# Mixer of a language-model tower: order of the second norm's root, the residual update and the sums behind the inverse

## The reference, cut to what matters

```
h = tok(x)                                   # ends in a layer norm with weights gf, bf
h = h + attn(layernorm(h))                   # the mixer
h = h + ffn(layernorm(h))                    # starts with a layer norm and a Fourier transform over the tokens

def attn(x):                                 # x is already layernorm(h)
    xn = (x - mean(x)) / sqrt(var(x) + 1e-5) * gamma + beta
    q, k, v = split(xn @ w_qkv)              # 16 features each
    q_l, k_l = means of 4 tokens of q, k     # 64 landmarks a sequence
    a1, a2, a3 = softmax(q k_l'), softmax(q_l k_l'), softmax(q_l k')
    z = a2' / (max column sum * max row sum)
    6 times: z = 0.25 z (13 I - a2 z (15 I - a2 z (7 I - a2 z)))
    out = a1 z (a3 v) + conv33(v)            # a convolution over tokens with 33 taps
    return x + out @ w_out + b_out
```

## Time and profile before

| | |
|---|---|
| three runs, us | 1111.16, 1113.62, 1119.43 (median 1113.62) |
| the profiled execution, us | 1112.04 |
| its span, first to last instruction, us | 1110.2 |
| TensorE busy | 973.0 us, 88% |
| VectorE, ScalarE, GpSimd busy | 606.5, 592.3, 426.6 us |
| mean granted TensorE clock | 0.927 of full |
| the mixer | from 491 to 604 us |

### The profile page before, as it was taken

One profiled execution on the slowest core, in us unless ns is written; L12 is line 12 of the kernel. 1 busy time (PEld: TensorE's weight loads), 2 busy tenths in 40 slices (PEclk: granted clock), 3 DMA queues, 4 the chain that ended last, 5 costly groups with the idle time before them and its releaser, 6 DMA issues. The chain is left out here.

```text
span 1110.2 us, 21063 instructions
## 1 busy us (share of the span) xinstructions
PE 973.0 (88%) x7350; PEld 709.2 (64%) x7350; DVE 606.5 (55%) x1802; ACT 592.3 (53%) x1332; POOL 426.6 (38%) x622
## 2 busy tenths in 40 slices
PE   2489999999999998625897999996899999997898
PEld 1256666667666665313685767775688888885564
DVE  4366776666766774135353111116277777784773
ACT  4166776676666766216434543326455555543476
POOL 6426777766677676548003000014400000027300
PEclk9699999999999999866698899998799999996899
DMA  4755444645554440010100011010000010005841
GB/s 131 170 104 132 94 93 108 151 107 110 118 127 94 94 97 8 1 33 0 47 3 9 20 36 32 21 33 1 20 10 11 11 54 15 1 1 136 214 100 37
DMA packets 54416, 71.82 MB, mean 65 GB/s; under 512 B 9476, under 2 KB 46624, under 8 KB 50464
## 3 DMA queue, kind: packets, MB, share of 16 engines
q1 hardware_dynamic: 53160, 67.33, 26.1%
q0 software_dynamic: 1152, 3.15, 1.2%
HBM read 48.96 MB, written 17.56 MB: 60 GB/s over the span
## 5 line engine op out<-in xcount | busy, mean ns | idle before, releaser
L2232 DVE TENSOR_REDUCE t_nmax<-banks 128x2 f32<-128x512 f32 x256 | 166.6, 685 | 86.7 <-PE banks L2042 81.4
L2161 ACT ACTIVATE t_probs<-banks 128x512 f32<-128x512 f32 x256 | 144.8, 592 | 78.9 <-PE banks L2064 77.8
L2042 PE MATMUL banks<-t_packed 96*128 96x256 bf16 x512 | 90.9, 278 | 15.0 <-DMA t_packed<-t_qk_pairs 12.9
L2320 POOL TENSOR_SCALAR xhat<-t_rbuf,mv,rstd 128x128 f32<-128x128 f32 x128 | 100.1, 795 | 3.3
L2064 PE MATMUL banks<-t_packed 120*128 120x256 bf16 x512 | 92.0, 278 | 9.3 <-DMA t_packed<-t_mT 8.6
L2042 PEld LDWEIGHTS banks<-t_packed 96*128 96x128 bf16 x512 | 47.4, 99 | 55.0 <-issue 27.1
L858 ACT ACTIVATE hid<-banks,b 128x512 f32<-128x512 f32 x64 | 43.5, 686 | 69.0 <-PE banks L763 68.3
L2064 PEld LDWEIGHTS banks<-t_packed 120*128 120x128 bf16 x512 | 46.7, 99 | 48.2 <-issue 21.2
L1192 ACT ACTIVATE l_probs<-banks,l_shift 128x256 f32<-128x256 f32 x128 | 59.4, 472 | 28.5 <-DVE l_shift L1233 25.8
L2077 PE MATMUL banks<-t_probs,t_v 128*32 128x256 f32 x1024 | 73.6, 392 | 0.6 <-ACT t_probs L2161 0.6
L901 DVE SCALAR_TENSOR_TENSOR acc<-banks,gates,acc 128x128 f32<-128x128 f32 (+1 forms) x72 | 20.1, 343 | 97.8 <-PE banks L783 97.8
(11 more groups left out here) (376 smaller groups left out, 2090.2 us busy)
## 6 DMA issues: line engine op xcount, KB each, us to landing
t_qk_pairs<-t_parts SPq DMA_DIRECT2D x32, 384.0 KB, 2.4
t_packed<-t_qk_pairs SPq DMA_DIRECT2D x32, 384.0 KB, 5.5
t_packed<-t_qk_pairs SPq DMA_DIRECT2D x32, 256.0 KB, 6.0
t_packed<-t_qk_pairs SPq DMA_DIRECT2D x32, 128.0 KB, 6.6
w<-in_L_ffn_w SPq DMA_DIRECT2D x16, 256.0 KB, 2.6
t_packed<-t_mT SPq DMA_DIRECT2D x32, 96.0 KB
g_qk_pairs<-g_parts SPq DMA_DIRECT2D x8, 384.0 KB, 5.7
g_packed<-g_qk_pairs SPq DMA_DIRECT2D x8, 384.0 KB, 4.8
```

The lines of the kernel that those rows point to most:

```text
L2042: ins = pe.matmul(m.mbank[:, n % 3, i * S:(i + 1) * S], m.packed[0:MROW, 0, p, h, c + qt * P:c + (qt + 1) * P], m.packed[0:MROW, 1, p, h, ...
L2161: act.activation(m.probs[:, n % 6, :], m.sbank[:, n % 2, :], ACT.Exp).then_inc(sem["probs_ready"], 1)
L2232: dve.tensor_reduce(m.nmax[:, b, u // 4, 2 * hp:2 * hp + 2], m.mbank[:, n % 3, :].rearrange("p (i k) -> p i k", i=2), AX.X, ALU.max, negat ...
L2320: ins = pool.tensor_scalar(m.xhat[:, k, i, :], m.rbuf[:, k, i, :], m.mv[:, k, i, 0:1], m.rstd[:, k, i:i + 1], ALU.subtract, ALU.mult)
```

## The change

Four things, all in the mixer:

1. The two roots of the second norm are computed apart. In H, GpSimd computes only the one that ScalarE's N needs (4 columns instead of 8, L587 and L588 of the changed kernel). The other one, 1 + root, the product and the residual update move into a new item NR (L590 to L598), which stands behind H 3 for pairs 0, 1 and 2 and behind SC for pair 3.
2. VO is cut in two (VT, VO), and ScalarE doesn't wait for the weights before the first F: VT comes behind F 2, F 3 behind H 0. N, NT, QK and VW of the four pairs are interleaved anew.
3. CV 0, which stood between VW 0 and QK 1, moves in front of CV 1, shortly before the inverse.
4. Behind the inverse, Y and R alternate pair by pair, and X, DF and HP are interleaved anew.

```diff
-    order = [("VO",)] + [("F", g) for g in range(PAIRS)]
-    order += [("H", 0), ("H", 1), ("N", 0), ("NT", 0), ("H", 2), ("N", 1), ("QK", 0), ("VW", 0), ("NT", 1), ("H", 3), ("N", 2), ("N", 3),
-              ("L", 0), ("CV", 0), ("QK", 1), ("NT", 2), ("NT", 3), ("S2", 0), ("L", 1), ("M2", 0), ("E2", 0), ("VW", 1),
-              ("QK", 2), ("QK", 3), ("A2", 0), ("S2", 1), ("L", 2), ("M2", 1), ("AT", 0), ("E2", 1), ("S31", 0), ("S2", 2), ("L", 3),
+    order = [("F", 0), ("F", 1), ("F", 2), ("VT",), ("H", 0), ("F", 3), ("VO",), ("H", 1), ("N", 0), ("NT", 0), ("H", 2), ("N", 1),
+             ("QK", 0), ("NT", 1), ("VW", 0), ("H", 3), ("NR", 0), ("NR", 1), ("NR", 2), ("N", 2), ("QK", 1), ("NT", 2), ("L", 0), ("N", 3), ("VW", 1),
+             ("S2", 0), ("QK", 2), ("NT", 3), ("L", 1), ("M2", 0), ("E2", 0), ("QK", 3),
+             ("A2", 0), ("S2", 1), ("L", 2), ("M2", 1), ("AT", 0), ("E2", 1), ("S31", 0), ("S2", 2), ("L", 3),
...
-              ("A2", 2), ("AT", 2), ("S31", 2), ("M31", 1), ("A2", 3), ("AT", 3), ("E31", 1), ("M31", 2), ("SC",), ("ET", 0), ("S31", 3),
-              ("E31", 2), ("M31", 3), ("VW", 2), ("CV", 1), ("E31", 3), ("VW", 3), ("ET", 1), ("P", 0), ("Z0",)]
+             ("A2", 2), ("AT", 2), ("S31", 2), ("M31", 1), ("A2", 3), ("AT", 3), ("E31", 1), ("M31", 2), ("SC",), ("NR", 3), ("ET", 0), ("S31", 3),
+             ("E31", 2), ("M31", 3), ("VW", 2), ("CV", 0), ("CV", 1), ("E31", 3), ("VW", 3), ("ET", 1), ("P", 0), ("Z0",)]
...
-    order += [("W2", g) for g in range(PAIRS)] + [("Y", g) for g in range(PAIRS)]
-    order += [("R", 0), ("R", 1), ("X", 0), ("R", 2), ("X", 1), ("DF", 0), ("DF", 1), ("R", 3), ("DF", 2), ("DF", 3), ("X", 2),
-              ("HP", 0), ("HP", 1), ("X", 3), ("DF", 4), ("DF", 5), ("DF", 6), ("HP", 2), ("DF", 7), ("HP", 3), ("HN",)]
+    order += [("W2", g) for g in range(PAIRS)]
+    order += [("Y", 0), ("R", 0), ("Y", 1), ("R", 1), ("X", 0), ("Y", 2), ("R", 2), ("Y", 3), ("X", 1), ("DF", 0), ("DF", 1), ("R", 3), ("X", 2),
+              ("DF", 2), ("DF", 3), ("HP", 0), ("X", 3), ("DF", 4), ("DF", 5), ("HP", 1), ("DF", 6), ("DF", 7), ("HP", 2), ("HP", 3), ("HN",)]
...
         @block.scalar
         def _(act):
-            act.wait_ge(sem["mix_rows_loaded"], 32)
...
                 elif kind == "NT":
+                    if g == 0:
+                        act.wait_ge(sem["mix_rows_loaded"], 32)
...
                 elif kind == "H":
                     pool.wait_ge(sem["x_stats"], g + 1)
-                    chain.step(pool.tensor_tensor(xrs[:, g], xve[:, g], half8[:, :, :], ALU.pow))
-                    pool.tensor_tensor(xnb[:, g], xnb[:, g], xrs[:, g], ALU.mult).then_inc(sem["x_rstd"], 1)
-                    chain.step(pool.tensor_scalar(xs1[:, g, :], xrs[:, g, 0, :], 1.0, None, ALU.add))
-                elif kind == "N":
-                    pool.wait_ge(sem["x_rstd"], g + 1)
+                    chain.step(pool.tensor_tensor(xrs[:, g, 1], xve[:, g, 1], half8[:, 1, :], ALU.pow))
+                    pool.tensor_tensor(xnb[:, g, 1], xnb[:, g, 1], xrs[:, g, 1], ALU.mult).then_inc(sem["x_rstd"], 1)
+                elif kind == "NR":
+                    chain.step(pool.tensor_tensor(xrs[:, g, 0], xve[:, g, 0], half8[:, 0, :], ALU.pow))
+                    pool.tensor_scalar(xs1[:, g, :], xrs[:, g, 0, :], 1.0, None, ALU.add)
+                    chain.step(pool.tensor_tensor(xnb[:, g, 0], xnb[:, g, 0], xrs[:, g, 0], ALU.mult))
                     pool.wait_ge(sem["n_ready"], g + 1)
```

More of the change, by code:

```diff
@@ L208, in _ @@
                 kind, g = item[0], item[-1]
-                if kind == "VO":
-                    bank = use(item)
+                if kind == "VT":
+                    bank = use(("VO",))
                     pe.wait_ge(sem["mix_w_loaded"], 32)
                     pe.transpose(bank[0:DK, 0:P], wqkv[:, 2 * DK:3 * DK], m.ident[:, :]).then_inc(sem["vo_turned"], 1)
+                elif kind == "VO":
+                    bank = bank_of(item)
                     pe.wait_ge(sem["vo_copied"], 1)
@@ L348, in _ @@
         def _(act):
[L349 removed]
             for item in order:
                 kind, g = item[0], item[-1]
[L352 removed]
+                if kind == "VT":
                     act.wait_ge(sem["vo_turned"], 1)
[L354 removed]
+                    act.activation(wvT[:, :], bank_of(("VO",))[0:DK, 0:P], ACT.Copy).then_inc(sem["vo_copied"], 1)
+                elif kind == "VO":
                     act.wait_ge(sem["vo_turned"], 2)
```

2 lines of the change are left out of this document (removed), and 2 rows, old and new, of the table order.

## The result

| | before | changed |
|---|---|---|
| median of 17 runs each, us | 1116.05 | 1110.31 (1103.41 to 1116.83) |
| ratio to before | | 0.9952, 95% interval 0.9935 to 0.9969 |
| profiled execution, us (span) | 1112.04 (1110.2) | 1105.52 (1103.7) |
| mixer, first VectorE instruction to last copy, us | 112.37 | 106.24 |

The change saves 0.5%, 5.4 us of 1116, where 0.7% was forecast. It is less than the 1% that the forecast took as telling, but the interval leaves out 1. The 1110.31 lies at the upper end of the range, 1101.5 to 1110.5. The mixer is 6.13 us shorter. The other 0.4 us between the two spans are differences of the stages around it: those ahead took 2.94 us less, those behind 2.55 more.

The account below looks back on a forecast made before the run. In the mixer's front no engine is full: a chain of waits, much with TensorE at its lower clock. Terms 2.0 - 0.3 + 5.1 = 6.8 us saved give 1105.2 or 1106.8; forecast 1106.0 us, range 1101.5 to 1110.5.

Parts of the forecast that it names:

- the sum: Whole mixer: start of the inverse, contention and tail added, 2.0 - 0.3 + 5.1 = 6.8 us saved.
- the front: Norms and projections up to pair 3's k: earlier roots and no wait of N3 bring k 4.3 us earlier.
- the chain behind it: Landmark, A2 and AT work after pair 3's k: keeps its order and moves by the same 4.3 us.
- CV 0: Convolution moved before the inverse: costs 3.62 us at the lower clock, 2.05 at the upper; inverse starts 2.0 us earlier.
- contention: Inside the inverse: GpSimd's update of pair 3 disturbs VectorE beside it, 0.3 us lost, bounds 0 and 1.2.
- the tail: Behind the inverse: sums and statistics pair by pair bring the last copy 5.1 us earlier, between 4.2 and 6.0.
- A rise a turn sooner: In the front: if TensorE's clock rises a turn sooner, pair 3's k comes 5.2 us earlier.
- F3 is late next: Start of the front: F3 stands ahead of N0, so of 2.6 us won only 0.2 are left.
- (a): Rival, only the tail pays: front's gain goes into CV0 and contention, 2.9 us saved in all; chance 0.20.
- (b): Rival, the clock helps everywhere in the mixer: 10.0 us saved, 1102.0 to 1103.6; chance 0.14.
- (c): Rival, slower: GpSimd not free behind the all-reduce, CV3's sum waits, up to 7 us slower, 1119; chance 0.04.

Follow-up runs that it names:

- e6: The changed kernel with N 0 moved ahead of F 3 in the order, nothing else; ratio 0.9906 to the kernel before.
- e2: The changed kernel with the old order behind the inverse, so the new front only; ratio 1.0004 to the kernel before.
- e5: The changed kernel with the convolution of pair 0 back in the front, behind L 0; ratio 0.9922 to the kernel before.
- e3: The changed kernel with GpSimd's clearing of the padded buffers moved to the mixer's start; ratio 0.9943 to the kernel before.
- e7: The changed kernel with 12 extra transposes on TensorE in its pause ahead of QK 3; ratio 0.9945 to the kernel before.
- e10: The changed kernel with 12 extra transposes ahead of QK 3 and the buffers cleared at the mixer's start; ratio 0.9923 to the kernel before.
- e17: The changed kernel once more, unaltered (its second execution); ratio 0.9959 to the kernel before, mixer 104.84 us.
- e8: The changed kernel with VT, VO and the wait for weights ahead of the four F, F 3 ahead of H 0; ratio 0.9874, two runs.
- e1: The kernel before with only the new order behind the inverse, so the tail only; ratio 0.9961 to the kernel before.
- e14: The changed kernel with N 0 ahead of F 3, CV 0 ahead of QK 3, extra transposes at the inverse's start; ratio 0.9899.

## Why the prediction was right or wrong

**The time.** 4.3 us lie between 1106.0 and 1110.31. Of these, 2.4 are the reference: the kernel before had a median of 1116.05 here, 1113.62 in the three runs of the forecast. The rest is the saving, 5.4 to 5.7 us measured against 6.8 by the sum and 7.6 from the median. In the two profiled executions the mixer was 6.1 and 7.5 us shorter; the sum was near, but of its terms only the tail was right for its reason. Term by term, in us saved against the forecast, in the first execution: the front 0.2 fewer, the chain behind it 1.7 fewer (its loss was put at nothing), CV 0 1.3 more, contention 0.1 fewer, the tail 0.1 more, together 6.1 instead of 6.8.

**The front, 4.3 forecast, 4.1 measured with the late rise of the clock and 5.7 with the early one: right in size, half right in cause.** (A rise a turn sooner was priced at 5.2.) N 3 without a wait, GpSimd's updates ending where they did (525.3 on the old axis, 525 forecast), F 0 on time. "Of the 2.6 us won at the start 0.2 are left; F3 is late next" was right as a fact (-0.1 measured), and stopped short: that F 3 in this place makes N 0 later than need be, which by e6 costs 2.5 us at the all-reduce, stands in the forecast's own sum (N 0 behind F 3) and wasn't priced.

**"The landmark, A2 and AT chain behind it keeps its order and moves by the same amount": this step failed.** 4.1 us at the last k were 2.39 at the all-reduce (in e2 5.7 were 2.65). The order was kept, the speed was not. Before, the clock had fallen at 26.8 and risen again at 33.6, so that TensorE did S31 0 and 1 at the upper level; now, with a pause of 1.7 us ahead of QK 3, it does them at the lower one (in e5 too, with CV 0 in the front again). Lying beside it was the clearing. The prediction had GpSimd's updates end where they did before, and with them the clearing behind; it moved VectorE's chain 4.3 us up and did not ask what it would meet. The scaling of A2 1 moved from 38.56 to 34.33, into the clears that stand from 33.89 to 36.22. e3, e7 and e10 show that both causes have to be removed, and then 1.84 us come back, where 1.7 were lost. The prediction priced the clock for VW, QK, CV and DF and left it out of the chain in between; contention it priced only behind the all-reduce.

**CV 0, 2.3 forecast, 0.98 measured: luck.** VW 2 to VW 3 took 5.28 before and 6.26 after. The rise was expected at 5.3 us behind the dense work's start, as before, and so CV 0 wholly at the lower level. The clock rose about 3.6 us behind VW 2's start, amid the first of the pair, and the second was cheap. That moment belongs to the execution: with the same items there it came 3.4 us behind VW 2 in e17 and 6.0 in e8, where VW 2 to VW 3 took 7.44, near the 7.6 of the forecast. At equal rises CV 0 costs 1.8, by e5. This error and the last one, 1.7 against 1.3, nearly cancel, and that is luck too.

**Contention, 0.3 forecast, bounds 0 to 1.2.** One VectorE step on one element took 1.18 us beside the addition of pair 3, and 0.43 of it reached the inverse (VW 3 to its first step took 2.49 before, 2.92 after); in the second execution the step took 0.54, and nothing reached the inverse (2.41). In size it was right; the same kind of meeting stood 20 us earlier at 1.94 us, where the prediction didn't look. The Trainium skill (SBUF — State Buffer, Who interferes with whom) names tensor_scalar, which the scaling is, among the VectorE instructions that can enter a mode in which either engine blocks the other for a whole instruction. The trace agrees, and goes beyond it (below).

**The tail, 5.1 forecast: right.** 5.16 and 5.94 measured, within the 4.2 and 6.0 given for a clock that falls and one that stays. In e17 it stayed; in the first execution it fell, but only 1.4 us behind the start of DF 0 and not in the pause ahead of it. X 0 3.02 us earlier behind the first sum (3.12 forecast), R 3 at 587.6 on the old axis (587).

**The rivals.** (a), only the tail pays, is what e1 and e2 show of the time, with the tail at its full size and not at its bound (the saving, 5.4 to 5.7 us, lies in the band of the forecast, 5 to 9, and not in that of (a)). (b) would have needed an upper clock in the front. It was argued down with "the front has no pause of 6.5 us", which its own rows contradict: TensorE stood 15.75 us in the earlier trace rows and 9.14 in the earlier trace rows. So the 0.64 of the front says nothing on short pauses; that the clock falls there all the same is what e6 and the others showed. e14 saved 11.9 us of the mixer, the size of (b), but with another list and extra work on TensorE. (c) did not come: GpSimd stood 7.55 us behind the all-reduce, far below the 31 up to which nothing was to be lost.
